# Matmuls of a constant between TensorE's steps, and new order tables, in a three-part block (scan, attention, mixture of experts) for four images

## The chip, the cores and the metric

One core of one Trainium2 chip. The time is the device time of one launch in microseconds (us). The kernel takes four images from one device memory to the other in a software pipeline, so one number covers the whole of it.

## What is computed

Per image (16 x 16 tokens of 192 channels) three stages follow one another:

```python
x = x + scan_block(gn(x))            # in_proj 192->2*96, 3x3 depthwise conv, SiLU, x_dbl, dt, softplus,
                                     # selective scan on 4 paths x 96 channels x 16 states, norm, gate, out_proj
t = to_tokens(x)                     # (4, 256, 192)
t = t + causal_attention(ln(t))      # 12 heads of 16: "l = 0" below
t = t + ffn_block(ln(t))             # full attention, 12 heads ("l = 1"), then a gelu MLP 192->768->192,
                                     # then 4 experts 192->768->192, the two best weighted by a softmax
```

The scan of one path and channel is `h = h * exp(d_t * A) + d_t * u_t * B_t; y = (h * C_t).sum()` for 256 steps, over 16 states.

## The kernel before

**Five blocks.** The program is a pipeline over images with three stages: the scan part (`ssm`), both attentions, and the feed-forward part (`ffn`: MLP is expert 0, the experts are 1 to 4). `OPENING` runs the scan of image 0 alone (0 to 114 us in the trace). `FIRST` runs the attentions of image 0 with the scan of image 1 (114 to 281). `STEADY` is a loop body that runs twice (281 to 466 and 466 to 653): attentions of one image, the scan of the next, the feed-forward of the one before. `LAST` has attentions and feed-forward (653 to 771), `CLOSING` feed-forward alone (771 to the end). Each block ends with a barrier of all engines.

**What sets the order.** Each engine works strictly through its own program. The attention is written out as the backbone: for l = 0 and l = 1 the slots are `"turned"`, `"projected"`, 0 to 11 (two for each of six units of two heads), `"context"`, `"spread"`, `"output"`. Tables `OPENING`, `FIRST`, `STEADY`, `LAST`, `CLOSING` say, for each engine and slot, which steps of the scan and of the feed-forward are put in there. Semaphores make a step wait for its inputs; a step whose inputs are late holds all that stands behind it on that engine.

**The attention backbone on TensorE (PE).** Transposes of `h_tok` (L766); slot `"turned"`; the projection of queries, keys and values (L773, 16 records of 96x256 and 8 of 128x192); stacks of high and low parts (L1105, 32 rows); slot `"projected"` between the fourth and fifth stack. Then for each unit u: `scores(u+1)` (L1130, 48 rows, and a mask, L1139), `row_max(u)` (L1148), `context(u-1)` (L1184), slot 2u, `shifted(u)` (L1160 and a mask, L1169), after u = 2 and 4 `spread` (L1193), slot 2u+1. After the units: `"context"`, `spread`, `"spread"`, the output projection (L1216), `"output"`. Between these stand the row maxima on VectorE (DVE, L1621), the copy into `q_stack` (L1634) and the exponentials on ScalarE (ACT, L1854 for l = 0, L1859 for l = 1), which TensorE waits for.

**The steps put into the slots.** `x_dbl` (L914), `dt` (L927), `y_sum(g)` (L964: 12 groups, each waits for the product with C on GpSimd, POOL, `times_C(g)`, L1916), `ffn_up` (L1020 to L1024), `ffn_down` (L1036), `ffn_turn` (L766, L1005). On DVE `silu` (L1332 to L1339) makes `xs`, which `x_dbl(0)` waits for through a POOL copy (L1905); `ffn_norm(0)` on DVE begins with the sum of `v` and the MLP's result (L1505).

**The bank `py`.** It belongs to the scan part. `y_sum` adds into its partitions 0 to 95.

Of the kernel before, what the change touches and what calls it, by code (L numbers as in the profile page):

```python
# [88 lines left out]
        (1, 1): [("y_sum", 2), ("y_sum", 3)],
        (1, 2): [("y_sum", 4)],  # L90
        (1, 4): [("y_sum", 5)],
        (1, 5): [("y_sum", 6), ("y_sum", 7), ("y_sum", 8)],
        (1, 6): [("y_sum", 9)],
        (1, 7): [("y_sum", 10)],
# [29 lines left out]
        (0, 2): [("in_proj",)],  # L124
        (0, 6): [("x_dbl", 0)],
        (0, 8): [("x_dbl", 1)],
        (0, "context"): [("softplus", 0)],
        (0, "spread"): [("softplus", 1), ("softplus_log",)],
        (0, "output"): [("decays", 0)],
# [39 lines left out]
        (1, "turned"): [("ffn_down", 1, 1), ("ffn_up", 3, 0), ("y_sum", 0)],  # L169
        (1, "projected"): [("y_sum", 1), ("ffn_down", 2, 0)],  # L170
        (1, 0): [("ffn_up", 3, 1)],
        (1, 1): [("y_sum", 2), ("y_sum", 3), ("ffn_down", 2, 1)],
        (1, 2): [("y_sum", 4)],
        (1, 3): [("y_sum", 5)],
        (1, 4): [("y_sum", 6)],
        (1, 5): [("ffn_up", 3, 2), ("y_sum", 7), ("ffn_down", 3, 0), ("ffn_down", 3, 1), ("y_sum", 8)],
# [1871 lines left out]
```

How the kernel before makes its waits and increments, by code:

```python
            def link(ins):  # L625
                count[0] += 1
                ins.then_inc(chain, 1)
                eng.wait_ge(chain, count[0])
# [54 lines left out]
            @block.gpsimd  # L683
            def _(pool):
                nc.gpsimd.memset(half[:], -0.5)
                nc.gpsimd.memset(ident[:], 0.0).then_inc(pool_set, 1)
                pool.wait_ge(pool_set, 1)
                nc.gpsimd.affine_select(out=ident[:, :], in_=ident[:, :], compare_op=ALU.not_equal, fill=1.0,
                                        base=0, pattern=[[-1, 128]], channel_multiplier=1).then_inc(pool_set, 1)
# [24 lines left out]
        def scan_constants(pool, link):  # L714
            link(nc.gpsimd.memset(sel[:], 0.0))
            for n in range(STATE):
                ins = nc.gpsimd.affine_select(out=sel[:, :], in_=sel[:, :], compare_op=ALU.not_equal, fill=1.0,
                                              base=GROUPS - 1 - GROUPS * PACK * n,
                                              pattern=[[-1, INNER + GROUPS - 1]], channel_multiplier=GROUPS)
                if n < STATE - 1:
                    link(ins)
            ins.then_inc(consts, 1)
            pool.wait_ge(consts, 2)
# [97 lines left out]
                @block.sync  # L822
# [7 lines left out]
                    if run_s:  # L830
                        sp.wait_ge(xd_copied, 2)
                        for dst, first in ((B_rows, RANK), (C_rows, RANK + STATE)):
# [14 lines left out]
                        if opening:
                            sp.wait_ge(dx_out, 16)
                            for g in range(1, GROUPS):
```

## Time and profile before

| | us |
|---|---|
| median of 3 runs (lowest, highest) | 841.64 (838.44, 844.35) |
| the profiled execution, its own time | 845.55 |
| its span, first to last instruction | 843.8 |
| PE busy in the span | 641.1 (76%) |
| DVE busy | 543.0 (64%) |
| ACT busy | 324.0 (38%) |
| POOL busy | 209.3 (25%) |

The profile page gives the busy time of each engine, and the span in 40 slices; the line PEclk in it is the clock granted to TensorE in tenths of its full 2.4 GHz (a 5 is 1.2 GHz). In the trace a row is one group of like instructions: start, length, engine, line, output and inputs, how many, and in brackets how long the engine had been idle before it and what ended that. A float32 matmul has two records, an fp32r or bf16 one has one. Lengths of matmuls contain a modelled end, so the distance from one start to the next tells more than a length.

### The profile page before, as it was taken

The page shows a single profiled execution, that of the slowest core. Times are in us where ns is not written, and L with a number is a line of the kernel's source. Part 1 is how long each engine was busy: PE and PEld are TensorE (multiplying, and loading weights), DVE is VectorE, ACT ScalarE, POOL GpSimd, SP SyncE. Part 2 cuts the span into 40 slices and gives each one's busy share as a digit, 9 for nine tenths or more (in the row PEclk, how much of TensorE's full clock was granted, in tenths as well). Part 3 has the DMA queues.
Part 4 walks back from the last instruction along what each step waited for, and adds up shares of the span by engine and source line. Part 5 has one row for each costly group of instructions (what it writes and reads, how often), then busy time and mean ns, then how long its engine had stood idle before and what let it go on. Part 6 is the DMA issues. An engine that isn't in the chain of part 4 may idle for free. (4 is left out here: it accounts for less than half of the span.)

```text
span 843.8 us, 8722 instructions
## 1 busy us (share of the span) xinstructions
PE 641.1 (76%) x3156; PEld 423.8 (50%) x3156; DVE 543.0 (64%) x938; ACT 324.0 (38%) x588; POOL 209.3 (25%) x184
## 2 busy tenths in 40 slices
PE   2379658956667778857798789777787889898697
PEld 2123235434223665635355656654354668766586
DVE  3749747568898566658897675668986455452211
ACT  2324122124432234554473324564471324462131
POOL 4419720212443210032352110133342111001000
PEclk9979956556799797879799986989898799898789
DMA  6986100237880004074750004195730000000000
GB/s 132 311 171 152 25 9 1 28 85 185 190 197 2 9 2 50 23 199 123 165 127 10 9 0 50 44 216 130 158 85 9 1 1 2 1 1 10 0 1 10
DMA packets 26641, 61.69 MB, mean 73 GB/s; under 512 B 4928, under 2 KB 12752, under 8 KB 26608
## 3 DMA queue, kind: packets, MB, share of 16 engines
q1 hardware_dynamic: 26608, 61.26, 31.8%
q8 instruction: 19, 0.31, 0.2%
q14 instruction: 14, 0.11, 0.0%
HBM read 53.52 MB, written 3.54 MB: 68 GB/s over the span
## 5 line engine op out<-in xcount | busy, mean ns | idle before, releaser
L1916 POOL TENSOR_TENSOR state<-state,C_rows 128x1024 f32<-128x1024 f32 x42 | 106.9, 2546 | 168.3 <-DVE state L1429 106.4
L964 PE MATMUL py<-state,sel 128*96 128x512 f32 x168 | 94.4, 692 | 38.4 <-POOL state L1916 38.4
L1036 PE MATMUL pd<-w_dn,act 128*128 128x192 f32 x480 | 88.6, 338 | 5.3 <-ACT act L1799 5.3
L1036 PEld LDWEIGHTS pd<-w_dn,act 128*128 128x128 f32 x480 | 82.0, 198 | 12.7 <-ACT act L1799 8.2
L1020 PE MATMUL pu<-fT,w_up 128*128 128x256 f32 x180 | 62.5, 432 | 10.5 <-ACT act L1799 8.7
L964 PEld LDWEIGHTS py<-state,sel 128*96 128x96 f32 x168 | 27.1, 178 | 82.5 <-POOL state L1916 51.0
L1957 POOL TENSOR_TENSOR cT<-cT,inv_den 128x256 f32<-128x256 f32 x24 | 20.2, 841 | 177.8 <-DVE inv_den L1646 177.8
L1429 DVE TENSOR_TENSOR_SCAN state<-decay,dx_rows 128x512 f32<-128x512 f32 x48 | 61.0, 1312 | 3.4 <-ACT decay L1769 1.9
L1799 ACT ACTIVATE act<-pu,b_up 128x256 f32<-128x256 f32 x90 | 37.8, 471 | 50.7 <-PE pu L1024 50.5
L1184 PE MATMUL pm<-probs,v_aug 128*32 128x256 f32 (+1 forms) x384 | 54.5, 411 | 3.1 <-DVE inv_den L1646 1.9
L1769 ACT ACTIVATE decay<-d_rows,a_neg 128x255 f32<-128x255 f32 x96 | 40.8, 498 | 40.3 <-DMA d_rows<-delta_dram 27.8
L1422 DVE TENSOR_TENSOR dx_rows<-dx_rows,B_rows 128x1024 f32<-128x1024 f32 x24 | 46.0, 1919 | 7.7 <-DMA dx_rows<-delta_x_dram 7.7
L1891 POOL TENSOR_TENSOR norm_rstd<-norm_var,half 128x2 f32<-128x2 f32 x20 | 14.0, 699 | 142.9 <-DVE norm_var L1242 142.9
L1646 DVE RECIPROCAL inv_den<-pm 128x256 f32<-128x256 f32 x24 | 42.1, 1754 | 10.6 <-PE pm L1193 10.4
L1854 ACT ACTIVATE probs<-ps 128x512 f32<-128x512 f32 (+1 forms) x48 | 20.9, 486 | 71.2 <-PE ps L1169 71.2
L1634 DVE TENSOR_TENSOR q_stack<-q_stack,ps 128x256 fp32r<-128x256 f32 x48 | 19.7, 410 | 42.0 <-PE ps L1148 41.9
L1022 PE MATMUL pu<-fT_high,w_up_stack 128*128 128x256 f32 x90 | 46.1, 512 | 0.0
L1130 PE MATMUL ps<-k_stack,q_stack 48*128 48x128 f32 (+1 forms) x192 | 26.3, 361 | 21.4 <-ACT k_stack L1839 8.9
L773 PE MATMUL ps<-hT,w_qkv 96*96 96x256 f32 x128 | 37.6, 459 | 5.9 <-DVE hT L1587 5.9
L1799 ACT ACT_TABLE_LOAD x31 | 39.8, 1283 | 0.6
L1020 PEld LDWEIGHTS pu<-fT,w_up 128*128 128x128 f32 x180 | 31.2, 210 | 16.2 <-ACT act L1799 10.3
L1859 ACT ACTIVATE probs<-ps 128x1024 f32<-128x1024 f32 x24 | 24.4, 1019 | 36.2 <-PE ps L1160 36.0
(294 smaller groups left out, 1300.5 us busy)
## 6 DMA issues: line engine op xcount, KB each, us to landing
dx_rows<-delta_x_dram SPq DMA_DIRECT2D x41, 512.0 KB, 5.2
d_rows<-delta_dram SPq DMA_DIRECT2D x36, 512.0 KB, 6.7
d_rows<-delta_x_dram SPq DMA_DIRECT2D x6, 512.0 KB, 5.2
w_dn<-exp_w_dram SPq DMA_DIRECT2D x1, 2304.0 KB
B_rows<-xdbl SPq DMA_DIRECT2D x4, 512.0 KB, 7.0
C_rows<-xdbl SPq DMA_DIRECT2D x4, 512.0 KB, 10.7
...
```

The costliest lines, as they stand in the source:

```text
L773: mm = nc.tensor.matmul(out, lhs(c), rhs(c), start=(c == 0), stop=(c == 1))
L964: mm = nc.tensor.matmul(py[0:INNER, :], sel[:, first:first + INNER], flat(states[g % held])[:, paths], start=False, stop=(g == GROUPS - 1) ...
L1020: nc.tensor.matmul(out, w_up[:, e, hidden], fT[:, :], start=True, stop=False)
L1022: nc.tensor.matmul(out, w_up_stack[:, e, hidden], fT_high[:, :], start=False, stop=False)
L1036: mm = nc.tensor.matmul(pd[:, WIDTH * tl:WIDTH * (tl + 1)], act[e % 2][:, m, 128 * tl:128 * (tl + 1)], w_dn[:, e, m, :], start=(m == 0), s ...
L1184: mm = nc.tensor.matmul(pm[row:row + 32, q0:TOKENS], v_aug[:, kt, head, :], probs[u % 2][:, j, kt, q0:TOKENS], start=(kt == 0), stop=(kt = ...
L1422: link(nc.vector.tensor_tensor(dx_rows[g % 2][:, :], dx_rows[g % 2][:, :], B_rows[:, :], ALU.mult))
L1429: ins = nc.vector.tensor_tensor_scan(flat(states[g % held])[:, both], flat(decay[g % 2])[:, both], dx_rows[g % 2][:, both], 0.0, ALU.mult, ...
L1646: nc.vector.reciprocal(inv_den[:, :], pm[:, TOKENS:2 * TOKENS]).then_inc(den_inv[l], 1)
L1769: ins = nc.scalar.activation(decay[g % 2][:, k, rest], d_rows[g % 2][:, k, rest], ACT.Exp, scale=a_neg[:, at:at + 1])
L1799: ins = nc.scalar.activation(act[e % 2][:, 2 * i + m, :], up_bank(e * HCH // 2 + i)[:, TOKENS * m:TOKENS * (m + 1)], ACT.Gelu, bias=b_up[: ...
L1916: nc.gpsimd.tensor_tensor(now, now, C_rows[:, :], ALU.mult).then_inc(sc_done, 1)
```

## The change

A new step `keep_busy(times)` on TensorE multiplies the constant `identb` (a 128 x 128 bf16 identity, here its columns 96 to 127 as the stationary operand) with itself four times over (512 columns), into partitions 96 to 127 of bank `py`. Nobody reads the result. It waits for nothing and signals nothing. It stands 228 times in the program as it is executed: 83 in `FIRST`, 54 in each of the two passes of `STEADY`, 37 in `LAST`, none in `OPENING` and `CLOSING`. In the same edit the tables of all engines in these three blocks are written anew. Line numbers grow by 13 in the early part of the file and by 22 or 23 behind the new function (L1184 is L1207, L1148 is L1171).

```diff
+                    def keep_busy(times):
+                        for _ in range(times):
+                            nc.tensor.matmul(py[INNER:128, :], identb[:, INNER:128],
+                                             identb[:, :].unsqueeze(1).to_broadcast([128, 4, 128]),
+                                             start=True, stop=True, tile_position=(0, INNER),
+                                             skip_group_check=True)
...
 STEADY = {
     "PE": {
-        (0, "turned"): [("ffn_turn", 0), ("x_turn",)],
+        (0, "turned"): [("keep_busy", 6), ("ffn_turn", 0), ("x_turn",)],
...
-        (0, 5): [("x_dbl", 1)],
+        (0, 5): [("keep_busy", 2), ("keep_busy", 3)],
...
-        (0, "spread"): [("ffn_down", 1, 0)],
-        (0, "output"): [("ffn_up", 2, 0), ("ffn_up", 2, 1), ("ffn_up", 2, 2)],
+        (0, "spread"): [("keep_busy", 7)],
+        (0, "output"): [("ffn_down", 1, 0), ("ffn_up", 2, 0), ("ffn_up", 2, 1), ("ffn_up", 2, 2)],
```

**TensorE in `FIRST`, from the last context sums of l = 0 to the projection of l = 1.** Before (the second row is `spread(2)`, the third the output projection, the last the projection of l = 1):

```order
L1184 MATMUL pm<-probs,v_aug 32x128
L1193 MATMUL pm<-cT,den_sel 128x256
L1216 MATMUL ps<-w_o,cT 128x192 x6
L766 MATMUL pm<-ident,h_tok 96x128
L766 MATMUL ps<-ident,h_tok 96x128
L766 MATMUL pm<-ident,h_tok 96x128
L766 MATMUL ps<-ident,h_tok 96x128
L773 MATMUL ps<-hT,w_qkv 96x256 x8
```

The same place of the changed kernel:

```order
L1207 MATMUL pm<-probs,v_aug 32x128
L896 MATMUL py<-identb 32x512 x5
L1216 MATMUL pm<-cT,den_sel 128x256
L1239 MATMUL ps<-w_o,cT 128x192 x6
L896 MATMUL py<-identb 32x512 x6
L779 MATMUL pm<-ident,h_tok 96x128
L779 MATMUL ps<-ident,h_tok 96x128
L779 MATMUL pm<-ident,h_tok 96x128
L779 MATMUL ps<-ident,h_tok 96x128
L896 MATMUL py<-identb 32x512 x9
L786 MATMUL ps<-hT,w_qkv 96x256 x8
```

Twenty matmuls of the constant stand now in front of four things that wait: `spread(2)`, the transposes and the projection.

**VectorE in `STEADY`, l = 0, from the copy into `q_stack` of unit 1 to the row maxima of unit 3.** Before:

```order
L1634 TENSOR_TENSOR q_stack<-q_stack,ps 128x256
L1505 TENSOR_TENSOR v<-pd,v 128x384
L1237 BN_STATS norm_raw<-v 128x6 x2
L1240 BN_AGGR norm_mv<-norm_raw 128x2 x2
L1242 TENSOR_SCALAR norm_var<-norm_mv 128x2
L1621 TENSOR_REDUCE top<-ps 128x2 x2
L1332 TENSOR_SCALAR state<-state 96x256
L1333 RECIPROCAL state<-state 96x256
L1334 TENSOR_TENSOR xs<-state 96x256
```

Now:

```order
L1657 TENSOR_TENSOR q_stack<-q_stack,ps 128x256
L1355 TENSOR_SCALAR state<-state 96x256
L1356 RECIPROCAL state<-state 96x256
L1357 TENSOR_TENSOR xs<-state 96x256
L1360 TENSOR_SCALAR state<-state 128x192
L1361 RECIPROCAL state<-state 128x192
L1362 TENSOR_TENSOR z_gate<-z_gate,state 128x192
L1528 TENSOR_TENSOR v<-pd,v 128x384
L1260 BN_STATS norm_raw<-v 128x6 x2
L1263 BN_AGGR norm_mv<-norm_raw 128x2 x2
L1265 TENSOR_SCALAR norm_var<-norm_mv 128x2
L1644 TENSOR_REDUCE top<-ps 128x2 x2
```

`silu` stands ahead of the sum with the MLP's result, and the row maxima of unit 2 (`top`) behind both.

**TensorE in `LAST`, l = 0, from `spread(0)` to `shifted(3)`.** Before (the rows of `shifted` begin with L1160):

```order
L1193 MATMUL pm<-cT,den_sel 128x256
L1130 MATMUL ps<-k_stack,q_stack 128x128
L1130 MATMUL ps<-k_stack,q_stack 128x256
L1130 MATMUL ps<-k_stack,q_stack 128x128
L1130 MATMUL ps<-k_stack,q_stack 128x256
L1139 MATMUL ps<-maskq,identb 128x128 x4
L1148 MATMUL ps<-ident,top 128x128 x2
L1184 MATMUL pm<-probs,v_aug 32x256
...
L1160 MATMUL ps<-q_stack,k_stack 128x256
```

Now:

```order
L1216 MATMUL pm<-cT,den_sel 128x256
L896 MATMUL py<-identb 32x512 x9
L1153 MATMUL ps<-k_stack,q_stack 128x128
L1153 MATMUL ps<-k_stack,q_stack 128x256
L1153 MATMUL ps<-k_stack,q_stack 128x128
L1153 MATMUL ps<-k_stack,q_stack 128x256
L1162 MATMUL ps<-maskq,identb 128x128 x4
L1171 MATMUL ps<-ident,top 128x128 x2
L1207 MATMUL pm<-probs,v_aug 32x256
...
L896 MATMUL py<-identb 32x512 x8
L1183 MATMUL ps<-q_stack,k_stack 128x256
```

Seventeen matmuls of the constant were put around the scores and in front of `shifted(3)`; nothing else moved in these rows.

## Rows read from the trace of the kernel before

**Rows 1.** The view of the cores: span and mean granted TensorE clock.

```profile
core 0: 843.8 us, clock 0.846
```

**Rows 2.** Busy time by stretch: engines with instruction counts, clock, DMA share, GB/s.

```profile
114.00:204.00 90.00, 65.36 (x288) 41.45 (x289) 59.98 (x109) 26.17 (x52) 19.06 (x17) 0.55 0.29 64
204.00:281.00 77.00, 53.19 (x216) 24.56 (x214) 66.23 (x82) 25.55 (x53) 31.60 (x16) 0.85 0.52 116
281.00:367.00 86.00, 71.06 (x431) 52.55 (x432) 54.12 (x131) 38.26 (x66) 10.00 (x13) 0.86 0.21 42
367.00:466.00 99.00, 75.11 (x347) 44.92 (x345) 83.07 (x98) 48.84 (x84) 33.51 (x17) 0.90 0.48 114
653.00:771.00 118.00, 105.55 (x669) 82.33 (x670) 56.69 (x125) 51.97 (x86) 10.86 (x14) 0.90 0.00 1
```

**Rows 3.** The same view for stretches in which the granted clock is 0.50.

```profile
134.30:176.00 41.70, 37.70 (x181) 21.25 (x177) 24.86 (x46) 8.66 (x19) 5.84 (x6) 0.50 0.21 26
...
315.20:328.90 13.70, 11.66 (x48) 6.16 (x48) 9.89 (x18) 1.34 (x3) 1.28 (x2) 0.50 0.37 43
339.10:345.90 6.80, 6.80 (x29) 4.28 (x27) 3.08 (x5) 2.19 (x4) 0.73 (x1) 0.50 0.01 2
369.80:380.10 10.30, 5.91 (x10) 2.91 (x11) 7.75 (x8) 7.25 (x13) 4.68 (x2) 0.50 0.71 171
499.50:520.00 20.50, 16.42 (x71) 9.77 (x68) 12.95 (x22) 4.12 (x8) 1.33 (x2) 0.50 0.42 51
...
653.10:663.40 10.30, 8.00 (x26) 6.09 (x27) 1.60 (x4) 2.86 (x5) 2.45 (x3) 0.50 0.00 0
```

**Rows 4.** The same view for twenty microseconds inside the first of these.

```profile
155.00:175.00 20.00, 20.00 (x93) 10.46 (x92) 7.94 (x15) 4.41 (x10) 2.40 (x3) 0.50 0.43 53
```

**Rows 5.** Timeline of PE: four bf16 masks and their follower, at either clock.

```profile
142.09 0.61 PE L1139 MATMUL ps<-maskq,identb 128*128 128x128 bf16 x4
142.49 0.63 PE L1148 MATMUL ps<-ident,top 128*128 128x128 f32 x2
...
688.50 0.40 PE L1139 MATMUL ps<-maskq,identb 128*128 128x128 bf16 x4
688.73 0.39 PE L1148 MATMUL ps<-ident,top 128*128 128x128 f32 x2
```

**Rows 6.** Timeline of PE: scores of following units, in FIRST and in LAST.

```profile
141.36 0.80 PE L1130 MATMUL ps<-k_stack,q_stack 48*128 48x128 f32 x4 [0.96 <-ACT probs L1854]
...
147.11 0.80 PE L1130 MATMUL ps<-k_stack,q_stack 48*128 48x128 f32 x4 [0.96 <-ACT probs L1854]
...
688.06 0.50 PE L1130 MATMUL ps<-k_stack,q_stack 48*128 48x128 f32 x4 [0.47 <-ACT probs L1854]
...
692.05 0.50 PE L1130 MATMUL ps<-k_stack,q_stack 48*128 48x128 f32 x4 [0.96 <-ACT probs L1854]
```

**Rows 7.** Timeline of PE in FIRST: projections of l = 0 and l = 1.

```profile
121.48 6.63 PE L773 MATMUL ps<-hT,w_qkv 96*96 96x256 f32 x16
...
175.96 1.22 PE L1193 MATMUL pm<-cT,den_sel 128*128 128x256 f32 x2 [0.54 <-DVE cT L1640]
180.38 4.21 PE L1216 MATMUL ps<-w_o,cT 128*128 128x192 f32 x12 [3.19 <-POOL cT L1957]
...
197.87 6.00 PE L773 MATMUL ps<-hT,w_qkv 96*96 96x256 f32 x16 [5.91 <-DVE hT L1587]
```

**Rows 8.** Timeline of DVE in FIRST: first low parts of l = 0.

```profile
128.59 0.47 DVE L1595 SCALAR_TENSOR_TENSOR q_stack<-ps,b_qk,q_stack 96x256 fp32r<-96x256 f32 x1
```

**Rows 9.** Timeline of DVE in STEADY: the sum with the MLP's result.

```profile
309.26 0.56 DVE L1505 TENSOR_TENSOR v<-pd,v 128x384 f32<-128x384 f32 x1 [2.51 <-PE pd L1036]
```

**Rows 10.** Timeline of PE in STEADY: projection, x_dbl(0), then y_sum(0) and projection of l = 1.

```profile
284.89 3.62 PE L773 MATMUL ps<-hT,w_qkv 96*96 96x256 f32 x16
...
315.81 1.94 PE L914 MATMUL py<-xs,w_x 96*44 96x256 f32 x4 [2.65 <-POOL xs L1905]
...
374.19 3.73 PE L964 MATMUL py<-state,sel 128*96 128x512 f32 x4 [6.37 <-POOL state L1916]
377.71 4.79 PE L773 MATMUL ps<-hT,w_qkv 96*96 96x256 f32 x16
```

More of the change, by code:

```diff
@@ L81 @@
     "PE": {
-        (0, "turned"): [("x_turn",), ("group_sums",)],
-        (0, 0): [("in_proj",)],
-        (0, 5): [("x_dbl", 0)],
+        (0, "turned"): [("keep_busy", 7), ("x_turn",), ("keep_busy", 6), ("group_sums",)],
+        (0, "projected"): [("in_proj",)],
+        (0, 4): [("x_dbl", 0)],
+        (0, 5): [("keep_busy", 1), ("keep_busy", 6)],
         (0, 7): [("x_dbl", 1)],
-        (0, 9): [("dt", 0)],
+        (0, 9): [("dt", 0), ("keep_busy", 1)],
+        (0, 10): [("keep_busy", 3)],
         (0, 11): [("dt", 1)],
+        (0, "context"): [("keep_busy", 3), ("keep_busy", 2)],
+        (0, "output"): [("keep_busy", 5), ("keep_busy", 1)],
+        (1, "turned"): [("keep_busy", 1), ("keep_busy", 8)],
         (1, "projected"): [("y_sum", 0), ("y_sum", 1)],
[L89 to L94, printed above, removed]
+        (1, 1): [("keep_busy", 1), ("y_sum", 2), ("keep_busy", 7), ("y_sum", 3), ("keep_busy", 1),
+            ("keep_busy", 4), ("y_sum", 4)],
+        (1, 3): [("keep_busy", 4)],
+        (1, 4): [("keep_busy", 4), ("keep_busy", 3), ("y_sum", 5), ("y_sum", 6)],
+        (1, 5): [("y_sum", 7), ("y_sum", 8), ("keep_busy", 6), ("keep_busy", 4)],
+        (1, 6): [("y_sum", 9), ("y_sum", 10)],
+        (1, 7): [("keep_busy", 5)],
         (1, 9): [("y_sum", 11)],
@@ L123 @@
     "ACT": {
[L124 to L129, printed above, removed]
+        (0, 1): [("in_proj",)],
+        (0, 4): [("x_dbl", 0)],
+        (0, 7): [("x_dbl", 1)],
+        (0, 11): [("softplus", 0), ("softplus", 1), ("softplus_log",)],
+        (0, "spread"): [("decays", 0)],
         (1, "turned"): [("decays", 1)],
@@ L168 @@
-        (0, "output"): [("ffn_up", 2, 0), ("ffn_up", 2, 1), ("ffn_up", 2, 2)],
[L169 to L176, printed above, removed]
@@ L177 @@
-        (1, 6): [("ffn_up", 4, 0)],
-        (1, 7): [("ffn_up", 4, 1), ("y_sum", 9)],
-        (1, 8): [("y_sum", 10), ("ffn_up", 4, 2)],
+        (0, "spread"): [("keep_busy", 7)],
+        (0, "output"): [("ffn_down", 1, 0), ("ffn_up", 2, 0), ("ffn_up", 2, 1), ("ffn_up", 2, 2)],
+        (1, "turned"): [("ffn_up", 3, 0), ("keep_busy", 1), ("ffn_down", 1, 1), ("keep_busy", 5),
+            ("keep_busy", 1), ("y_sum", 0)],
+        (1, "projected"): [("ffn_down", 2, 0), ("y_sum", 1)],
+        (1, 0): [("ffn_down", 2, 1), ("y_sum", 2)],
@@ L227 @@
         (1, 5): [("ffn_up", 4, 0)],
[L228 to L229 removed]
+        (1, 6): [("decays", 11)],
+        (1, 7): [("ffn_up", 4, 1)],
+        (1, 9): [("ffn_up", 4, 2)],
     },
     "POOL": {
[L232 to L235 removed]
@@ L236 @@
-        (1, 2): [("times_C", 8)],
-        (1, 6): [("ffn_norm", 1)],
-        (1, 7): [("times_C", 9), ("times_C", 10)],
-        (1, 8): [("times_C", 11), ("y_norm",)],
-        (1, 11): [("ffn_turn", 1)],
-        (1, "spread"): [("y_out",)],
+        (0, "turned"): [("ffn_turn", 0), ("group_sums",)],
+        (0, 1): [("ffn_norm", 0), ("silu",)],
+        (0, "output"): [("times_C", 0), ("times_C", 1)],
+        (1, "turned"): [("ffn_norm", 1)],
+        (1, "projected"): [("times_C", 2), ("times_C", 3), ("times_C", 4), ("times_C", 5), ("times_C", 6),
+            ("times_C", 7), ("times_C", 8)],
@@ L242 @@
+        (1, 3): [("times_C", 9), ("times_C", 10)],
+        (1, 4): [("times_C", 11)],
+        (1, 11): [("y_norm",)],
+        (1, "output"): [("ffn_turn", 1), ("y_out",)],
     },
@@ L246 @@
     "PE": {
-        (0, "turned"): [("ffn_turn", 0), ("ffn_up", 0, 0)],
+        (0, "turned"): [("ffn_turn", 0), ("keep_busy", 8), ("ffn_up", 0, 0)],
         (0, "projected"): [("ffn_up", 0, 1)],
@@ L293 @@
     "POOL": {
-        (0, "turned"): [("ffn_turn", 0), ("ffn_norm", 0), ("ffn_norm", 1)],
-        (0, 4): [("ffn_turn", 1)],
+        (0, "turned"): [("ffn_turn", 0)],
+        (0, 0): [("ffn_norm", 0), ("ffn_norm", 1)],
+        (0, "spread"): [("ffn_turn", 1)],
     },
```

152 lines of the change are left out of this document (80 added, 72 removed).

## The prediction

> **What bounds the kernel now.** I read the views in this order: the cores, the busy time by stretch, then the timeline of TensorE (PE) where it is slow. The mean granted clock is 0.846 [rows 1]. The clock has two levels, 1.2 and 2.4 GHz (0.50 and 1.00), so a mean of 0.846 says that 2 x (1 - 0.846) = 31% of the span, some 260 us, ran at the lower one. By stretch [rows 2]: in the first attention (l = 0) of FIRST the clock is 0.55 and PE is busy 65.36 of 90 us; in l = 0 of STEADY 71.06 of 86, with VectorE (DVE) at 54.12; in LAST 105.55 of 118. These are PE's stretches. In the second attention (l = 1) the scan's groups run, and DVE has 66.23 of 77 us in FIRST and 83.07 of 99 in STEADY: there a faster PE mostly waits longer. So the gain to be had lies in l = 0 of FIRST and of both STEADY passes, in LAST, and where one attention hands over to the next.
>
> The slow stretches [rows 3] follow a pause or narrow work, not an idle PE alone. From 155 to 175 PE is busy in all 20.00 us and stays at 0.50 [rows 4]; the work there is scores of 48 rows, masks, context sums.
>
> **The price of one matmul of the constant.** No row of before has it. It streams 512 columns of bf16, as much as four masks of 128. Four masks take 142.49 - 142.09 = 0.40 us from start to the follower's start at 1.2 GHz, and 688.73 - 688.50 = 0.23 at 2.4 [rows 5]. So one costs 0.23 to 0.40 us, and all 228 cost 52 to 91 us of PE. They are free only inside a wait. That is the sum's main risk: PE takes its program in order, and a matmul of the constant in front of a step that is due delays it.
>
> **The parts, each as a gain (+) or loss (-).** Where PE is the bound, work at 0.50 costs twice what it costs at 1.00, so half its busy time is the most a stretch can give.
>
> *FIRST, start.* Thirteen stand around the x transposes. The projection of l = 0 (6.63 us at 121.48, [rows 7]) could take 3.62 as in [rows 10]. But its low parts wait for DVE, which starts on them at 128.59 [rows 8], about when the projection ends; DVE's chain before that is not shortened. 0 (bounds -2 and +3).
>
> *FIRST, units of l = 0.* PE 37.70 of 41.70 us [rows 3]. One unit takes 147.11 - 141.36 = 5.75 us at 0.50, and 692.05 - 688.06 = 3.99 at 1.00 [rows 6]: 1.8 saved in each. But no matmul of the constant stands before slot 5, so the first units stay as they are. Behind it lies about the stretch of [rows 4]: half of 20.00 is 10, and DVE with 7.94 doesn't forbid it. Off go seven at 0.40 in slot 5 and four at 0.23 later, 3.7. That leaves 6.3; part of it goes before the clock is up. in_proj moves forward to "projected", into a gap, worth about 1. Together +5 (0 to 11).
>
> *FIRST, hand-over.* The output projection could go from 4.21 us to half, +2.1; the projection of l = 1 from 6.00 to 3.62, +2.4, of which I count half since DVE must keep up. Five in front of spread(2) take 1.2 where the wait was 0.54 [rows 7]: -0.7. The six and nine behind (3.5 to 6 us in two places) fit in the wait of 5.91 and the one before the transposes. +3 (-1 to +4.5).
>
> *STEADY, silu ahead of the sum with v.* DVE stood idle 2.51 us for the sum [rows 9] while silu could have run; PE then waited 2.65 for xs [rows 10]. silu now fills that gap. What is late next: the row maxima of unit 2, behind both; so not all of 2.51 comes back. I take 1.5 in each pass, +3 (0 to 5). Without that gap on DVE it would be worth nothing.
>
> *STEADY, units of l = 0.* The two slow stretches at the same place have PE 11.66 and 16.42 [rows 3]; half is 14.0, and DVE was idle in them 13.70 - 9.89 and 20.50 - 12.95, in sum 11.4, which caps it. The fall came with the wait for xs, which shrinks, and five matmuls of the constant follow spread(0). I take half of 14.0, less 8 x 0.23 a pass, partly under waits: +5 (-3 to +11). Stretch 339.1: 6.80, half 3.4; I take +1.5.
>
> *STEADY, hand-over.* y_sum(0) waits 6.37 us for POOL, the clock falls, and then it takes 3.73 and the projection 4.79 [rows 10]. With one and six in that wait (1.6 to 2.8 us, it fits), y_sum can take half, +1.9, the projection 3.62, +1.2: 3.1 in the first pass, and I take 2 in the second. Seven ahead of the output projection (1.6) stand in the place of an ffn_down that now runs behind it, where PE waits for ScalarE anyway: -1. Together +4 (0 to 6).
>
> *STEADY, "turned".* Six in front of ffn_turn and x_turn. In the first pass PE has no wait from there to the projection, and the clock is low: 6 x 0.40 = 2.4; in the second 1.4, part under the wait for x. An earlier rise gives something back. -2 (-4 to 0).
>
> *LAST.* At 653.1 PE is busy 8.00 of 10.30 at 0.50 [rows 3]: +4 at most, less 8 x 0.40 = 3.2 against 2.3 of idle time: +2. Then seventeen around unit 3 cost 3.9 at 2.4 GHz, against waits of 0.47 and 0.96 [rows 6]: -2.5. Later short slow stretches may give 1 to 2. 0 (-5 to +6).
>
> *l = 1 of FIRST and STEADY.* 39 and 26 matmuls stand there, 9 and 6 us at 0.23; PE has 77 - 53.19 and 99 - 75.11 = 24 us idle [rows 2]. 0. The cover is DVE's and POOL's scan work; if it were gone they would cost those 9 and 6 us.
>
> Sum: 0 + 5 + 3 + 3 + 5 + 1.5 + 4 - 2 + 0 = 19.5 us. From the profiled execution's 845.55 us (span 843.8, 1.75 around it) that gives 826.0. It was 3.9 above the median of 841.64, so against the median I expect 822.
>
> **A rule weighed against the trace.** The row that matters for how the clock is got back is [rows 4]: PE busy without a break, clock at 1.2 GHz throughout. The Trainium skill, "TensorE: Matmul & The Clock Gate", section "Why this matters for your kernels", advises to keep TensorE busy continuously to get the full clock. This case's trace does not agree that being busy is enough. By the page any filler would do, and the bounds above, 11 + 4.5 + 11 + 6, would be the likelier values; by the row it depends on which work fills the time. The constant's matmuls take 128 rows, as does the y_sum at 374.19 [rows 10], with which the clock came back at 380.1 [rows 3], so I expect them to help; but they write 32 partitions only, as the context sums do.
>
> The same page, Part 3, section "What overlaps and what doesn't", says that matmuls start and end in program order. No row here shows an exception; by it nothing behind a matmul of the constant can pass, and the losses above stand in full.
>
> **Rivals.**
> - *The clock rises, but the gain goes into waits.* For it: in l = 0 of STEADY DVE has 54.12 of 86 us and each unit passes PE, DVE, PE, ACT in turn; even at full clock a unit has ACT waits of 0.47 and 0.96 [rows 6]. Against it: 20 us with PE busy throughout [rows 4]. A quarter of the clock terms (14.5 x 0.25 = 3.6) and silu's 3, less 2: 5 us, 837. Chance 0.22.
> - *More than I count.* The new tables let the units and DVE follow, and most upper bounds are reached: 11 + 4.5 + 5 + 11 + 3.4 + 6, less 2 = 39; 803. Against it: DVE must be free at the right times. Chance 0.14.
> - *Slower: the constant does not hold the clock.* Then they do as little for it as the context sums at 155 to 175, and those in PE's own stretches are pure cost. Of them 7 + 4 + 5 in FIRST, 6 + 8 + 7 in each STEADY pass and 8 + 17 + 12 in LAST, 95 in all, are at most half under waits; 48 x 0.40 = 19 us, less silu's 3: 16 us, 858. It decides from the point where uncovered matmuls cost more than the clock gives; with 0.23 to 0.40 each that is about 50 of them with no clock gained. Against it: they take all 128 rows. Chance 0.14.
>
> **How the numbers follow.** The forecast, 810 to 833, has 0.50. A measurement of this kernel can tell about 1% (8.4 us) from no change. Faster by more is the forecast and the second rival: 0.64. Within 1%: the first rival, 0.22. Slower: 0.14. The range 805 to 846 leaves out the slower case (0.14) and the far end of the second rival (0.06).
>
> **What would show it.** In the trace of after the mean granted clock should go from 0.846 to 0.90 or more; the hand-over of FIRST should show the output projection at 2.2 us and the projection at 3.6; x_dbl(0) of STEADY should wait under 1 us for xs; the stretches of l = 1 should keep their length. I am wrong if the clock is at 0.50 behind rows of the constant (third rival), or if it is high and the waits for DVE and ACT in l = 0 grew by as much (first rival).

## The result

The changed kernel takes 817.46 us (median of 4, 817.37 to 822.21) against 841.2 us (838.44 to 844.35) for the kernel before beside it: a ratio of 0.9736, 95% interval 0.9688 to 0.9784. Run again later it took 822.77 against 839.6, ratio 0.9801 (0.975 to 0.9853). So the gain is 17 to 24 us by the medians. I had forecast 19.5, and 822; the result is 4.5 us from it and inside the range. Ratios leave disturbed executions out (one, of the last experiment below, took 1529.9 us), while the medians beside them are of all.

The views of the changed kernel, first the cores and then the page's groups, with the row of the constant:

```profile
core 0: 815.8 us, clock 0.902
```

```profile
PE 660.2 (81%) x3384; PEld 425.5 (52%) x3384; DVE 540.3 (66%) x938; ACT 323.0 (40%) x588; POOL 209.2 (26%) x184
...
L896 PE MATMUL py<-identb 128*32 128x512 bf16 x228 | 64.1, 420 | 0.0
```

The mean clock went from 0.846 [rows 1] to 0.902. PE's busy time rose from 641.1 to 660.2 us, though the 228 matmuls alone have records of 64.1: what was there before takes less time. None of the 228 waits for anything (0.0 us idle before them).

Busy time by stretch, of the changed kernel, with the stretches cut where the work itself turns: from the start of an attention's projection to the start of its output projection (FIRST l = 0 and 1, l = 0 and 1 of both STEADY passes, LAST l = 0). Columns: length, then busy time of PE, PEld, DVE, ACT and POOL with counts, the clock, DMA share, GB/s.

```profile
120.90:171.30 50.40, 40.66 (x256) 24.12 (x255) 37.03 (x69) 14.75 (x31) 8.97 (x9) 0.80 0.17 22
188.20:268.90 80.70, 64.52 (x260) 28.69 (x260) 69.84 (x79) 27.29 (x58) 33.52 (x16) 0.86 0.50 127
278.80:341.40 62.60, 55.46 (x362) 38.06 (x360) 43.56 (x107) 28.10 (x50) 5.81 (x8) 0.92 0.13 16
365.80:445.80 80.00, 71.73 (x354) 43.75 (x352) 70.89 (x82) 45.43 (x76) 30.51 (x15) 0.94 0.47 113
456.60:519.20 62.60, 55.40 (x362) 37.96 (x360) 43.50 (x107) 28.08 (x50) 5.74 (x8) 0.92 0.13 16
543.70:623.80 80.10, 71.38 (x354) 43.55 (x352) 71.02 (x83) 45.31 (x76) 30.52 (x15) 0.94 0.44 112
635.40:681.90 46.50, 43.73 (x323) 31.66 (x321) 26.82 (x66) 18.55 (x37) 3.86 (x5) 0.96 0.00 1
```

The same seven stretches of the kernel before:

```profile
121.50:180.40 58.90, 50.48 (x240) 30.16 (x240) 39.68 (x69) 14.92 (x31) 12.66 (x11) 0.56 0.15 19
197.90:275.20 77.30, 55.12 (x221) 25.22 (x221) 70.19 (x79) 27.44 (x57) 33.48 (x16) 0.85 0.58 131
284.90:351.20 66.30, 57.37 (x359) 40.62 (x357) 43.24 (x106) 27.18 (x49) 5.77 (x8) 0.85 0.13 17
377.70:461.30 83.60, 68.56 (x327) 41.36 (x325) 70.77 (x79) 42.03 (x72) 30.45 (x15) 0.92 0.45 108
469.90:538.60 68.70, 59.66 (x358) 42.94 (x356) 42.47 (x103) 27.12 (x49) 5.14 (x7) 0.80 0.12 15
562.40:648.60 86.20, 70.07 (x328) 41.43 (x326) 71.39 (x81) 42.51 (x74) 30.50 (x15) 0.91 0.47 106
661.10:709.40 48.30, 43.27 (x310) 32.41 (x310) 27.01 (x66) 19.41 (x39) 3.85 (x5) 0.94 0.01 1
```

Read the lengths: -8.5, +3.4, -3.7, -3.6, -6.1, -6.1, -1.8, in sum 26.4 of the 28.0 us between the two spans. This is one execution of each. Two things do not fit my steps: l = 1 of STEADY, put at 0, gave 9.7 us, and the largest single difference, l = 0 of FIRST, turns out below to be no work of the matmuls of the constant. A second profile of the changed kernel (820.2 us) has the lengths of l = 1 of STEADY again, 81.20 and 79.90, but in l = 0 of STEADY it is slower:

```profile
281.00:344.90 63.90, 55.53 (x361) 38.21 (x359) 43.41 (x106) 27.98 (x50) 5.69 (x8) 0.92 0.13 16
...
462.20:529.50 67.30, 58.91 (x361) 40.70 (x359) 43.50 (x107) 28.00 (x50) 5.78 (x8) 0.85 0.12 14
```

So of the 9.8 us of these two stretches (62.60 twice for 66.30 and 68.70) only 3.8 are there in the second profile.

What a matmul of the constant costs is seen in the timeline of PE, in FIRST behind spread(0). Columns: start, length, instruction, [idle time before].

```profile
151.45 3.07 PE L896 MATMUL py<-identb 128*32 128x512 bf16 x7
154.44 0.50 PE L1153 MATMUL ps<-k_stack,q_stack 48*128 48x128 f32 x4
...
237.91 2.33 PE L896 MATMUL py<-identb 128*32 128x512 bf16 x10
240.18 0.51 PE L1153 MATMUL ps<-k_stack,q_stack 48*128 48x256 f32 x4
```

Seven in 2.99 us to the follower's start are 0.43 each; ten at the full clock take 2.27, 0.227 each. The forecast's price, 0.23 to 0.40, is right at one end and a little low at the other. Behind the seven the scores take 0.50 us, as at 2.4 GHz in [rows 6], while in the profile of before this part of the attention ran at a clock of 0.50 [rows 4].

### The profile page after: what moved, and what is told of

Same layout as the page of the kernel before. It is cut to its first block and busy times, and to the rows that moved or that the text cites. A ratio compares the mean times of both kernels' runs of the same rounds, so it can differ in the third digit from the quotient of the medians.

```text
span 815.8 us, 9176 instructions
## 1 busy us (share of the span) xinstructions
PE 660.2 (81%) x3384; PEld 425.5 (52%) x3384; DVE 540.3 (66%) x938; ACT 323.0 (40%) x588; POOL 209.2 (26%) x184
## 5 line engine op out<-in xcount | busy, mean ns | idle before, releaser
L1939 POOL TENSOR_TENSOR state<-state,C_rows 128x1024 f32<-128x1024 f32 x42 | 108.7, 2588 | 158.6 <-DVE state L1452 98.5
L986 PE MATMUL py<-state,sel 128*96 128x512 f32 x168 | 92.0, 680 | 26.0 <-POOL state L1939 26.0
L1059 PE MATMUL pd<-w_dn,act 128*128 128x192 f32 x480 | 90.7, 343 | 4.9 <-ACT act L1822 4.9
L1452 DVE TENSOR_TENSOR_SCAN state<-decay,dx_rows 128x512 f32<-128x512 f32 x48 | 64.3, 1381 | 0.8
L896 PE MATMUL py<-identb 128*32 128x512 bf16 x228 | 64.1, 420 | 0.0
L1043 PE MATMUL pu<-fT,w_up 128*128 128x256 f32 x180 | 59.2, 412 | 3.7 <-ACT act L1822 3.7
L1207 PE MATMUL pm<-probs,v_aug 128*32 128x256 f32 (+1 forms) x384 | 47.7, 368 | 2.4 <-ACT probs L1882 1.1
L1445 DVE TENSOR_TENSOR dx_rows<-dx_rows,B_rows 128x1024 f32<-128x1024 f32 x24 | 43.9, 1830 | 5.0 <-DMA dx_rows<-delta_x_dram 5.0
L1045 PE MATMUL pu<-fT_high,w_up_stack 128*128 128x256 f32 x90 | 43.9, 488 | 0.0
L896 PEld LDWEIGHTS py<-identb 128*32 128x32 bf16 x228 | 21.0, 103 | 35.7 <-issue 21.2
```

Source lines behind the costliest of these rows:

```text
L896: nc.tensor.matmul(py[INNER:128, :], identb[:, INNER:128], identb[:, :].unsqueeze(1).to_broadcast([128, 4, 128]), start=True, stop=True, t ...
L986: mm = nc.tensor.matmul(py[0:INNER, :], sel[:, first:first + INNER], flat(states[g % held])[:, paths], start=False, stop=(g == GROUPS - 1) ...
L1043: nc.tensor.matmul(out, w_up[:, e, hidden], fT[:, :], start=True, stop=False)
L1045: nc.tensor.matmul(out, w_up_stack[:, e, hidden], fT_high[:, :], start=False, stop=False)
L1059: mm = nc.tensor.matmul(pd[:, WIDTH * tl:WIDTH * (tl + 1)], act[e % 2][:, m, 128 * tl:128 * (tl + 1)], w_dn[:, e, m, :], start=(m == 0), s ...
L1207: mm = nc.tensor.matmul(pm[row:row + 32, q0:TOKENS], v_aug[:, kt, head, :], probs[u % 2][:, j, kt, q0:TOKENS], start=(kt == 0), stop=(kt = ...
```

## The experiments

None of the kernels below leaves out any of the reference's computation. The kernel before ran beside each.

**Orders alone.**

```diff
-                        for _ in range(times):
+                        for _ in range(0):
```

> The changed kernel with keep_busy emptied, so the new order tables stand alone. My theory (the constant's matmuls bring about 16 to 20 us by way of the clock, the orders about 3 by silu ahead of the sum with v): 836 to 839 us, mean granted clock 0.84 to 0.86, the wait of x_dbl(0) for xs in STEADY under 1 us. Rival (the orders do the work and the constant's matmuls little): 818 to 824 us.

Measured: 832.3 us against 835.41, ratio 0.9877 (0.9799 to 0.9956). The new tables without any matmul of the constant are worth about 1%, some 10 us by the ratio (the interval allows 4 to 17), where I had expected 836 to 839. Its profiled execution was 11 us above its median, so little is built on its lengths.

**Matmuls of the constant alone.** The tables of before, with all 228 matmuls at the places that answer to the changed kernel's (STEADY shown; FIRST and LAST likewise).

```diff
-        (0, "turned"): [("ffn_turn", 0), ("x_turn",)],
+        (0, "turned"): [("keep_busy", 6), ("ffn_turn", 0), ("x_turn",)],
...
-        (0, 5): [("x_dbl", 1)],
+        (0, 5): [("keep_busy", 5), ("x_dbl", 1)],
...
-        (0, 9): [("dt", 0)],
+        (0, 9): [("dt", 0), ("keep_busy", 3)],
...
-        (0, "spread"): [("ffn_down", 1, 0)],
+        (0, "spread"): [("ffn_down", 1, 0), ("keep_busy", 7)],
```

> The kernel before with its own tables, and the 228 matmuls of the constant put at the corresponding waits. My theory: the clock goes to 0.89 to 0.90 and the time to 822 to 828 us, since silu's move (3 us) and the fitting of the tables to the new clock are missing. Rival (only both together gain): 835 us or more, at whatever clock.

Measured: 840.39 against 835.41, ratio 1.0055 (1.001 to 1.010). The view of the cores:

```profile
core 0: 841.5 us, clock 0.890
```

The clock is up by almost as much as in the changed kernel, and the kernel is no faster, if anything a little slower; I had expected 822 to 828. In the total this looks like my first rival, a higher clock that gains nothing. But it is not waits that swallow the gain: PE is busy 671.1 us of 841.5, where it was 641.1 of 843.8, so its idle time fell from 202.7 to 170.4 us, and the matmuls of the constant themselves fill what was won. The first stretch of STEADY, l = 0:

```profile
276.60:346.80 70.20, 62.31 (x374) 42.41 (x372) 44.05 (x107) 27.96 (x50) 5.76 (x8) 0.83 0.12 16
```

It took 66.30 us before, with 57.37 busy at 0.85. The clock isn't up here, PE is busy 4.9 us longer, and its idle time is 7.9 us for 8.9.

**The same on 32 rows.** The changed kernel, with the constant's matmuls cut from 128 rows to 32: the same number, the same 512 columns.

```diff
-                            nc.tensor.matmul(py[INNER:128, :], identb[:, INNER:128],
-                                             identb[:, :].unsqueeze(1).to_broadcast([128, 4, 128]),
+                            nc.tensor.matmul(py[INNER:128, :], identb[0:32, INNER:128],
+                                             identb[0:32, :].unsqueeze(1).to_broadcast([32, 4, 128]),
```

> The changed kernel with the constant's matmuls on 32 rows of the array in place of 128; number, columns and partitions written stay. If what the stream occupies decides whether it holds the clock: mean clock back at 0.84 to 0.87 and 838 to 850 us (their time is paid for nothing). If any matmul that keeps TensorE busy will do: 0.90 and 816 to 819 us.

Measured: 851.21 against 835.41, ratio 1.0182 (1.0104 to 1.026), clock 0.865. The page's row of these matmuls shows that they take PE no less time than in the changed kernel (70.4 us of records for 64.1, at the lower clock):

```profile
L896 PE MATMUL py<-identb 32*32 32x512 bf16 x228 | 70.4, 449 | 0.0
```

So keeping PE occupied is not what helps. The edit changes a second thing with the rows, though: rows 0 to 31 of `identb` are zero in columns 96 to 127, so here the stationary operand is all zeros, where on 128 rows it holds the 32 ones of the identity. Whether the rows decide or the zeros is not separated by any run. This is the slower rival as it would have come with a weaker constant.

**FIRST, second attention, without its 39.**

```diff
                         for name, *at in steps("PE", slot):
+                            if name == "keep_busy" and plan is FIRST and slot[0] == 1 and slot[1] in range(12):
+                                continue
                             work[name](*at)
```

> The changed kernel without the 39 matmuls of the constant in slots 0 to 11 of l = 1 in FIRST. That attention took 80.7 us from its projection to its output projection, 77.3 before, and VectorE waited 3.8 us for a row_max that stood behind ten of them. My theory: they are in the way there; the stretch falls back to 77 to 78 us and the kernel to 814 to 816 us. Rival: without them the clock falls more often in that stretch, the y_sums take twice as long, and the kernel is at 818 to 822 us.

Measured: 820.91 against 835.41, ratio 0.9805 (0.9742 to 0.9868). That can't be told from the changed kernel, and the 814 to 816 us that I expected did not come. The stretch went from 80.70 to 77.1 us, as expected, but it is also 77.9 in the second profile of the changed kernel, and 75.7 to 81.3 over six profiles with the 39 in place, so no gain or loss of theirs is shown.

**STEADY, first attention, without its 21.** The same two lines, with `plan is STEADY and slot[0] == 0`. It was sent with the changed kernel itself.

> The changed kernel itself once more, as the yardstick for the three that are sent with it. Every theory expects 817 to 822 us and a mean clock of 0.902; if it lies at 812 or 828 on this chip, the others are read against it and not against 817.

> The changed kernel without the 21 matmuls of the constant in the first attention of STEADY (the six in turned included); its tables stay. Theory (the reordered tables alone bring nothing there, the two are needed together): l = 0 of STEADY goes from 62.6 to 69 us or more in each pass, as in orders_only (72.8 and 70.4), the total 10 to 16 us up. Rival (what makes orders_only slow there is the low clock that it brings along from FIRST): l = 0 stays at 62 to 65 us, and the total within 4 us of the changed kernel.

Measured: 830.78 us (ratio 0.9887, 0.9836 to 0.9938) beside 822.77 (0.9801) for the changed kernel: 8.0 us more, less than the 10 to 16 expected, and the intervals overlap slightly. As the theory said, l = 0 of STEADY took 72.2 and 69.1 us, where the changed kernel has 62.60 in both passes of its first profile and 63.90 and 67.30 in that of this call. Of all the places tried, these 42 executed matmuls cost most when they are taken away.

**The two together.** Why do they bring nothing in the tables of before? In those x_dbl(1) stands right behind spread(0), and so behind the five matmuls; in the changed kernel it stands two slots later. The timeline of PE in the kernel with the matmuls alone:

```profile
313.09 2.32 PE L893 MATMUL py<-identb 128*32 128x512 bf16 x5
315.34 1.50 PE L933 MATMUL py<-xs,w_x 96*44 96x256 f32 x4
318.26 0.50 PE L1150 MATMUL ps<-k_stack,q_stack 48*128 48x128 f32 x4 [1.43 <-ACT probs L1874]
```

and of ScalarE, in the same kernel:

```profile
316.87 0.59 ACT L1739 ACTIVATE xdbl<-py 44x512 f32<-44x512 f32 x1 [12.74 <-PE py L933]
317.37 0.84 ACT L1874 ACTIVATE probs<-ps 128x512 f32<-128x512 f32 x2
```

The copy of x_dbl(1) stands ahead of the unit's exponentials there, so these wait until PE is through the five matmuls and x_dbl(1), and PE then pauses 1.43 us for them. With one step moved on three engines,

```diff
+STEADY["PE"][0, 5] = [("keep_busy", 5)]
+STEADY["PE"][0, 7] = [("x_dbl", 1), ("ffn_up", 1, 0), ("ffn_logits",)]
+STEADY["DVE"][0, 7] = [("ffn_turn", 1), ("ffn_logits",), ("ffn_turn_gates",)]
+STEADY["DVE"][0, 10] = [("x_dbl", 1)]
+del STEADY["ACT"][0, 3]
+STEADY["ACT"][0, 10] = [("x_dbl", 1)]
```

ScalarE starts the exponentials while PE runs the five (316.72 to 318.97 there):

```profile
315.87 0.87 ACT L1882 ACTIVATE probs<-ps 128x512 f32<-128x512 f32 x2 [8.11 <-PE ps L1197]
```

> fill_only (the tables of before, the 228 matmuls of the constant) with one step moved: the second x_dbl of STEADY from the place right behind the five matmuls of the constant to the next slot but one, on PE, DVE and ACT, as in the changed kernel. Theory (in fill_only this step and its copies stand ahead of unit 3 and spread(0) to spread(1) takes 20.1 us instead of 15.2): l = 0 of STEADY goes from 70 to 65 to 66 us in both passes, the total some 9 us below fill_only, near 831. Rival (the loss is spread over several of the moved steps): 69 to 71 us stay, the total 838 to 842.

Measured: 835.81 against 833.89, ratio 0.9993 (0.9944 to 1.0041), where the one without the move had 1.0055: half a per cent, some 5 us by the ratios, less than the 9 expected; their intervals overlap a little. In the profile l = 0 of STEADY went from 70.2 and 70.1 to 64.60 and 67.50. The same stretch in six kernels shows it best, from spread(0) to spread(1) in STEADY, by windows, first pass (the second passes agree within 0.5 us, but for the kernel before with 21.00): in order the kernel before, the matmuls alone, the new tables alone (the changed kernel without its 21; x_dbl(1) is in its new place, and so are the other steps), both with x_dbl(1) as the only step moved, both in the changed kernel, and the changed kernel on 32 rows.

```profile
318.70:338.10 19.40, 17.08 (x103) 11.18 (x101) 11.24 (x34) 9.23 (x14) 0.73 (x1) 0.74 0.44 54
```

```profile
312.00:332.10 20.10, 17.82 (x108) 11.13 (x106) 11.20 (x34) 9.22 (x14) 0.72 (x1) 0.81 0.42 53
```

```profile
315.30:334.50 19.20, 18.22 (x100) 12.14 (x97) 10.45 (x33) 7.95 (x13) 0.73 (x1) 0.63 0.00 1
```

```profile
315.60:332.20 16.60, 15.87 (x108) 10.15 (x106) 11.11 (x34) 8.75 (x13) 0.73 (x1) 0.90 0.00 1
```

```profile
314.20:329.40 15.20, 15.20 (x104) 9.65 (x102) 10.43 (x33) 7.93 (x13) 0.73 (x1) 0.87 0.00 1
```

```profile
315.30:334.70 19.40, 19.40 (x104) 11.83 (x102) 10.40 (x33) 7.92 (x13) 0.73 (x1) 0.65 0.00 1
```

19.40 as it was, 20.10 with the matmuls alone, 19.20 with the new tables alone, 16.60 and 15.20 with both. Neither part is worth anything by itself. With the tables alone PE is busy 18.22 us, but at 0.63; with the matmuls alone the clock is 0.81, but PE still waits 2.28 us (2.32 before) and has the five to do besides. And on 32 rows PE is busy in all 19.40 us at 0.65: no shorter than without any matmul of the constant. That x_dbl(1) in its new place without the matmuls gains nothing in the tables of before was not run; the new tables stand for it.

**Orders of STEADY's second attention alone**, in the kernel before, no matmul of the constant (part of PE and the boundary of DVE and POOL shown; the rest and ACT likewise).

```diff
...
-        (1, 1): [("y_sum", 2), ("y_sum", 3), ("ffn_down", 2, 1)],
-        (1, 2): [("y_sum", 4)],
-        (1, 3): [("y_sum", 5)],
-        (1, 4): [("y_sum", 6)],
-        (1, 5): [("ffn_up", 3, 2), ("y_sum", 7), ("ffn_down", 3, 0), ("ffn_down", 3, 1), ("y_sum", 8)],
+        (1, 1): [("ffn_up", 3, 1), ("y_sum", 3)],
+        (1, 3): [("y_sum", 4), ("y_sum", 5)],
+        (1, 4): [("y_sum", 6)],
+        (1, 5): [("ffn_up", 3, 2), ("y_sum", 7), ("ffn_down", 3, 0), ("ffn_up", 4, 0), ("ffn_down", 3, 1)],
...
-        (0, "output"): [("scan", 0)],
-        (1, "turned"): [("ffn_add", 1), ("scan", 1)],
+        (1, "turned"): [("scan", 0), ("scan", 1), ("ffn_add", 1)],
...
-        (1, 6): [("ffn_norm", 1)],
+        (1, "turned"): [("ffn_norm", 1)],
```

> The kernel before with only the orders of STEADY's second attention taken from the changed kernel, on all engines, and no matmul of the constant anywhere. Theory (the 3.6 and 6.1 us that l = 1 of STEADY won are the orders', of the scan's steps against the rest, not the clock's; orders_only has 78.9 and 78.9 us there at a mean clock of 0.842): l = 1 of STEADY goes from 83.6 and 86.2 to 79 to 80 us in both passes, the rest keeps its lengths, the total 8 to 11 us below the kernel before. Rival (l = 1 was shorter in orders_only because the first attention before it left other work behind, or through the clock): 83 to 86 us as before, the total unchanged.

Measured: 829.15 against 833.89, ratio 0.9903 (0.9848 to 0.9958). Busy time by stretch, l = 1 of both STEADY passes:

```profile
370.00:448.90 78.90, 67.00 (x328) 41.51 (x326) 72.42 (x84) 45.43 (x76) 30.54 (x15) 0.94 0.49 119
...
549.80:628.80 79.00, 67.74 (x327) 41.78 (x325) 70.76 (x81) 45.54 (x76) 30.46 (x15) 0.93 0.47 113
```

78.90 and 79.00 us for 83.60 and 86.20: the whole difference of the changed kernel, at a clock that is 0.02 above the kernel before's. It holds over executions: with the old orders the stretch took 82.6 to 86.2 us in six passes of three profiles (with and without matmuls of the constant), with the new ones 78.9 to 81.2 in eighteen passes of nine (the kernel on 32 rows left aside). In the stretch's waits (us in total, how many, the longest) the scan chain shows it. Before:

```profile
POOL state L1916 <- DVE state L1429: 46.8, 11, 9.7
```

and with these orders:

```profile
POOL state L1977 <- DVE state L1490: 41.4, 11, 6.8
```

GpSimd waits 5.4 us less for VectorE's scans. ScalarE's decays waited 5.9 us for them before, and have no row of 2 us or more now. One move that fits this is scan(1), which stood behind the sum with expert 1's result and stands ahead of it now; which of the moved steps did it was not tried one by one. In the total 1% (some 8 us by the ratio, 4.7 by the medians) stands against 11.9 in the two stretches; the rest of STEADY varied by a few us between executions.

**STEADY without the six in "turned".** The two lines with `plan is STEADY and slot == (0, "turned")`.

> The changed kernel without the six matmuls of the constant ahead of ffn_turn and x_turn in STEADY (two passes, 12 in all). My prediction priced them at a loss of 2 us in sum. By it the total falls by 2 us and the stretch from the h_tok transposes to the projection by 1 to 2 us a pass. Rival (they lift the clock for the projection and the first units, by the fall of no_steady_l0): l = 0 of STEADY is 1 to 3 us longer in each pass, the total 2 to 6 us up.

Measured: 820.67 against 833.89, ratio 0.9814 (0.9766 to 0.9861), the changed kernel in its own calls 0.9736 and 0.9801. From the transposes to the projection it took 3.5 and 3.6 us instead of 3.6 and 5.2 (5.1 and 5.2 in the second profile of the changed kernel); l = 0 took 65.50 and 63.90, inside the 62.60 to 67.30 of the changed kernel. Neither the 2 us that I expected nor the rival's loss can be told by these runs.

**FIRST, first attention, without its matmuls of the constant.** There are 35 of them (the expectation says 34). The two lines with `plan is FIRST and slot[0] == 0`.

> The changed kernel without the 34 matmuls of the constant in the first attention of FIRST; its tables stay. l = 0 of FIRST went from 58.9 to 50.4 us, where I had predicted 5. Theory (most of it is the clock): l = 0 of FIRST at 54 to 56 us, the total 4 to 6 us up. Rival (it is the tables; orders_only has 53.2 us, and no_steady_l0 had 47.5 with the same 34 in place, so a few us there are chance of the clock): within 3 us of 50.4 and of the changed kernel.

Measured: 820.06 against 833.89, ratio 0.9788 (0.9727 to 0.9849): no difference. The stretch by windows, first in this kernel, then in the one with only STEADY's second attention changed, whose FIRST is the kernel before's to the letter:

```profile
123.30:170.90 47.60, 37.04 (x240) 23.24 (x240) 37.11 (x69) 14.71 (x31) 8.98 (x9) 0.79 0.18 23
```

```profile
121.00:171.70 50.70, 40.98 (x239) 26.00 (x239) 39.33 (x69) 14.76 (x31) 12.66 (x11) 0.70 0.17 21
```

The same tables that took 58.90 us at 0.56 in the profile before took 50.70 at 0.70 here, and the changed kernel's, without any of the 35, took 47.60. So the clock of this stretch differs from one execution to the next, by 8 us in its length. With the 35 in place the new tables took 47.5 to 52.7 us in six profiles, so the 47.60 without them is no loss, and the -8.5 us is not what the constant did.

**LAST without its 37.** The two lines with `plan is LAST`.

> The changed kernel without the 37 matmuls of the constant in LAST; its tables stay. My prediction set LAST at 0. By orders_only the first attention of LAST takes 50.1 instead of 46.5 us and the second 48.4 instead of 48.5, so the theory that they earn their cost expects the total 3 to 5 us up. Rival (they cost what they give): within 1.5 us of the changed kernel.

Measured: 826.88 (ratio 0.9862, 0.9809 to 0.9915) beside 822.77: 4.1 us more, as expected, but the intervals overlap. Busy time by stretch, its l = 0:

```profile
643.50:693.20 49.70, 45.16 (x301) 33.29 (x301) 27.00 (x66) 18.55 (x37) 3.84 (x5) 0.84 0.00 1
```

49.70 us at 0.84 for 46.50 at 0.96 (46.3 to 46.6 in six profiles with the 37 in place). Its l = 1 took 45.60 us, where it was 48.50 and 46.90, so a part of the 3.2 us comes back there.

**More of them.** The changed kernel with 37 more, in LAST's end and in the waits of CLOSING, which has none.

```diff
+LAST["PE"][1, "output"] = [("keep_busy", 8)]
+CLOSING["PE"][0, "turned"] = [("ffn_turn", 0), ("keep_busy", 5)]
+CLOSING["PE"][0, 1] = [("ffn_down", 0, 0), ("ffn_down", 0, 1), ("keep_busy", 22)]
+CLOSING["PE"][0, 6] = [("ffn_turn", 1), ("keep_busy", 5)]
```

> The changed kernel with 37 more matmuls of the constant: five more at the end of LAST, and 5, 22 and 5 in the waits of CLOSING, of which the longest is 5.43 us for f_tok. They all lie before waits that the trace of after shows (1.65, 1.38, 5.43, 1.31 us). Theory (rows streamed in a wait keep the clock up, and what follows has a run of TensorE work): the clock stays at 1.00 from 748 to 756 and from 761 to 779, the projections there take 1.05 -> 0.6 us each; LAST to the end 73.9 -> about 68, total 5 us less than the changed kernel. Rival (CLOSING is paced by VectorE and ScalarE there, as fill_only was): the clock is up, the length within 1.5 us of 73.9.

Measured: 822.06 us (ratio 0.9744, 0.967 to 0.9817) beside the changed kernel's 822.77 (0.9801, 0.975 to 0.9853). The intervals overlap; whether it is better stays open. The end of the program, from LAST's last output projection on, in the changed kernel's two profiles and in this one:

```profile
741.90:815.80 73.90, 56.59 (x290) 49.86 (x289) 13.93 (x45) 15.35 (x33) 3.15 (x4) 0.86 0.02 6
```

```profile
750.60:820.20 69.60, 51.41 (x291) 45.56 (x289) 13.93 (x45) 15.35 (x33) 3.15 (x4) 0.95 0.02 6
```

```profile
752.60:822.20 69.60, 58.90 (x327) 48.37 (x325) 13.93 (x45) 15.35 (x33) 3.16 (x4) 0.98 0.02 6
```

The theory had 73.9 going to 68, and it took 69.60 at 0.98. But the changed kernel itself did 69.60 in its second profile, at 0.95. No gain of these 37 is shown.

## Why the prediction was right, and where its steps were not

The total was within 5 us, and one of the two main places of the gain, first attentions that PE bounds at a low clock, was named. Several terms were missed, in both directions, and the errors cancelled: that the sum fits so well is luck.

- *What bounds the kernel, and that the constant lifts the clock:* right. The mean went to 0.902, where 0.90 was asked for. 128 rows do it and 32 rows, all zeros in the stationary operand, do not (0.865, and 1.8% slower), which bears on what I weighed against the Trainium skill, "TensorE: Matmul & The Clock Gate", section "Why this matters for your kernels": it advises to keep TensorE busy, and this case's windows, PE busy 19.40 of 19.40 us at 0.65 on 32 rows and 15.20 of 15.20 at 0.87 on 128, again do not agree that busy is enough. One reading there was wrong: the y_sum at 374.19, on 128 rows, ended at 377.71 with the clock still low; at 380.1 it was the projection, on 96 rows, that ran [rows 10]. And the first rival's clock terms, 14.5, leave out the +4 of STEADY's hand-over; with it that rival comes to 5.6 us, which changes nothing.
- *FIRST, units +5 and hand-over +3:* the profiles seem to confirm the first and more (-8.5). The experiment without the 35 shows no loss at all. The step that failed is "Behind it lies about the stretch of [rows 4]": I took a clock of 0.50 over 41.70 us of one execution for the kernel's habit. The hand-over: I had asked for an output projection of 2.2 us and a projection of 3.6. The timeline of PE in the changed kernel has neither:

```profile
171.33 3.89 PE L1239 MATMUL ps<-w_o,cT 128*128 128x192 f32 x12 [3.25 <-POOL cT L1980]
...
188.22 5.38 PE L786 MATMUL ps<-hT,w_qkv 96*96 96x256 f32 x16 [2.39 <-DVE hT L1610]
```

  They answer to 4.21 and 6.00 of [rows 7]. The wait of 3.25 us behind spread(2) is one that the five ahead of it don't cover, and nine in the wait for hT leave 2.39 of it. By windows the clock is 0.51 in the first 2 us of the output projection, and 0.56 and 0.54 from 188.20 to 192.00 in the projection; it is at 1.00 only from about the end of each.
- *STEADY, silu ahead of the sum, +3:* the gap was filled, and it was worth 0.6 us in the pass shown. VectorE's gap of 2.51 us [rows 9] and PE's wait of 2.65 for xs [rows 10] are gone, but the row maxima of unit 2, which I had named as late next, took most of it. Timeline of PE:

```profile
310.01 0.44 PE L1171 MATMUL ps<-ident,top 128*128 128x128 f32 x2 [2.13 <-DVE top L1644]
...
311.35 1.94 PE L936 MATMUL py<-xs,w_x 96*44 96x256 f32 x4
```

  PE waits 2.13 us there instead. The timeline of DVE, in the changed kernel and then before:

```profile
302.49 0.42 DVE L1657 TENSOR_TENSOR q_stack<-q_stack,ps 128x256 fp32r<-128x256 f32 x1 [1.00 <-PE ps L1171]
...
305.27 0.25 DVE L1360 TENSOR_SCALAR state<-state 128x192 f32<-128x192 f32 x1
...
308.94 1.01 DVE L1644 TENSOR_REDUCE top<-ps 128x2 fp32r<-128x256 f32 x2
```

```profile
306.33 0.42 DVE L1634 TENSOR_TENSOR q_stack<-q_stack,ps 128x256 fp32r<-128x256 f32 x1 [0.27 <-PE ps L1148]
...
310.86 1.01 DVE L1621 TENSOR_REDUCE top<-ps 128x2 fp32r<-128x256 f32 x2
...
315.01 0.25 DVE L1337 TENSOR_SCALAR state<-state 128x192 f32<-128x192 f32 x1
```

  The half of silu for z_gate (2.06 us, 305.27 to 307.33) stood behind xs before, where x_dbl(0) did not wait for it. It moved along, so 4.50 us of silu went into a gap of 2.51. From the copy of unit 1 the row maxima start after 308.94 - 302.49 = 6.45 us, where it was 310.86 - 306.33 = 4.53. x_dbl(0) starts after 311.35 - 302.49 = 8.86 us, where it was 315.81 - 306.33 = 9.48. That is 0.6 us gained for the 1.5 that I took. I had counted the gap and not the second half of silu. From the projection's start x_dbl(0) comes even later, 311.35 - 278.80 = 32.6 us for 315.81 - 284.89 = 30.9, since the copy of unit 1 is itself 2.2 us later there; what delays it is open.
- *STEADY, units +5, and stretch 339.1 +1.5:* right in kind, and in size as far as can be told (3.7 + 6.1 = 9.8 us in the first profile, 3.8 in the second), not in reason. I costed the matmuls and the moved orders as separate terms; the six windows above show that they are one. Taking the 21 away costs 8.0 us and the tables alone leave l = 0 at 72.2 and 69.1.
- *STEADY, hand-over +4:* y_sum(0) and the projection, in the timeline of PE:

```profile
362.38 3.65 PE L986 MATMUL py<-state,sel 128*96 128x512 f32 x4 [2.78 <-POOL state L1939]
365.82 3.67 PE L786 MATMUL ps<-hT,w_qkv 96*96 96x256 f32 x16
```

  The wait of 6.37 became 2.78 and the projection 4.79 became 3.67, but y_sum(0) stayed at the low clock (3.65 for 3.73). 1.2 us of the 3.1 came. In the second pass I can show no gain.
- *STEADY, "turned" -2:* no loss and no gain can be told.
- *LAST 0:* the matmuls there are worth 4.1 us by the medians, 3.2 in the stretch of l = 0. The step that failed is most likely the -2.5 for the seventeen around unit 3: I priced their 3.9 us against short waits and gave them nothing for the clock, which is 0.84 in this stretch without LAST's 37, and 0.96 with them. The seventeen were not taken out by themselves. Against the kernel before, tables included, the stretch gained 1.8 us (48.30 to 46.50).
- *l = 1 of STEADY 0:* this was the largest miss, 8 us or so. I read "DVE has 83.07 of 99 us" [rows 2] as a bound, and looked in the new tables only for what the 26 matmuls cost. 16 us of idle DVE is room for an order, and the order took 4.7 and 7.2 of it.
- *l = 1 of FIRST 0:* right, within what can be told.

By the totals: orders of l = 1 of STEADY some 8, matmuls in l = 0 of STEADY 8.0, in LAST 4.1, in FIRST and in "turned" nothing that can be told. Their sum of 20 us lies within the 17 to 24 measured; it is not a strict split, since each was measured against another base and each ratio is known to about 4 us either way, a difference of two of them to about 6.
